# A running sum per token in DRAM in place of a scatter buffer that is read back, in a decoder layer with a mixture of experts

## The reference, cut to what matters

```python
C = int(1.25 * S / E)                                   # 320
topk_pn = topk_p / jnp.sum(topk_p, axis=1, keepdims=True)
idx = buf[:, :C]; valid = idx < S                       # the tokens of each expert
xin = x_pad[idx]
h = jax.nn.relu(jnp.einsum('ecd,edh->ech', xin, w1) + b1[:, None, :])
out = jnp.einsum('ech,ehd->ecd', h, w2) + b2[:, None, :]
out = out * jnp.where(valid, tok_w, 0.0)[:, :, None]
final = jnp.zeros((S + 1, d), xf.dtype).at[idx.reshape(-1)].add(out.reshape(-1, d))[:S]
```

## Time and profile before

| | us |
|---|---|
| median of the runs (lowest, highest) | 564.18 (563.95, 564.62) |
| span of the profiled execution | 558.4 |
| PE, DVE, ACT, POOL busy | 447.8, 374.0, 247.2, 145.5 |
| expert stage, 410 to 495: PE, DVE, ACT, POOL busy | 82.4, 69.7, 77.2, 34.7 |
| last stage, 526 to 558: DVE, ACT, POOL busy | 17.8, 12.2, 17.3 |

### The profile page before, as it was taken

One profiled execution on the slowest core, in us unless ns is written; L12 is line 12 of the kernel. 1 busy time (PEld: TensorE's weight loads), 2 busy tenths in 40 slices (PEclk: granted clock), 3 DMA queues, 4 the chain that ended last, 5 costly groups with the idle time before them and its releaser, 6 DMA issues.

```text
span 558.4 us, 14892 instructions
## 1 busy us (share of the span) xinstructions
PE 447.8 (80%) x5408; PEld 353.1 (63%) x5408; DVE 374.0 (67%) x1572; ACT 247.2 (44%) x802; POOL 145.5 (26%) x207
## 2 busy tenths in 40 slices
PE   4989999898998998998989967621799999999100
PEld 3546777786886877877877856611567777777100
DVE  3656789557658666576575583678578898887074
ACT  0543366224223233233242232442399888883044
POOL 0121351113103102112121131104403444422475
PEclk9979799669559687586595585665699999999755
DMA  8940063110200100100101000010644555500292
GB/s 253 321 161 1 30 210 122 29 31 2 75 0 26 49 0 28 47 0 28 47 0 45 26 1 21 2 39 18 197 155 147 164 166 163 179 25 25 87 312 96
DMA packets 38241, 46.47 MB, mean 83 GB/s; under 512 B 4283, under 2 KB 32702, under 8 KB 38202
## 3 DMA queue, kind: packets, MB, share of 16 engines
q1 hardware_dynamic: 35002, 36.56, 20.4%
q0 software_dynamic: 3200, 9.40, 5.2%
HBM read 34.98 MB, written 11.01 MB: 82 GB/s over the span
## 4 chain that ended last, share of the span: by engine, by line
PE 48%; DVE 20%; ACT 14%; issue 10%; POOL 3%; DMA 2%; SPq 1%; ACTq 1%; DVEq 0%; POOLq 0%
PE bank L748 46%; ACT qp L566 3%; DVE ub L1098 2%; DVE h L1109 2%; ACT arena L657 2%; ACT kp L666 2%; ACT arena L666 2%; DVE h L1112 1%; DVE hist L1110 1%; DVE st L1173 1%; DVE tm L1141 1%; PE bank L1023 1%; DVE mb L1100 1%; ACT arena L695 1%; ACT nb L544 1%
## 5 line engine op out<-in xcount | busy, mean ns | idle before, releaser
L1098 DVE TENSOR_TENSOR_SCAN ub<-rzb,bank 128x32 f32<-128x32 f32 x128 | 28.0, 219 | 90.1 <-ACT rzb L541 89.4
L541 ACT ACTIVATE rzb<-bank 128x32 f32<-128x32 f32 x128 | 27.5, 215 | 131.8 <-PE bank L748 131.8
L748 PE MATMUL bank<-h,whp 128*128 128x16 f16 x1920 | 75.5, 176 | 4.0 <-DVE h L1112 2.6
L748 PEld LDWEIGHTS bank<-h,whp 128*128 128x128 bf16 x1920 | 61.0, 99 | 10.4 <-DVE h L1112 3.3
L748 PEld LDWEIGHTS bank<-hsb,at_w 66*64 66x64 f32 x256 | 31.9, 167 | 43.8 <-DVE hsb L1104 27.3
L748 PE MATMUL bank<-arena 128*128 128x320 f16 x384 | 57.3, 308 | 1.4 <-DVE arena L1488 1.4
L748 PE MATMUL bank<-arena,kp 128*128 128x320 f16 x384 | 54.5, 299 | 0.0
L748 PE MATMUL bank<-hsb,at_w 66*64 66x16 f32 x256 | 41.6, 240 | 14.0 <-DVE hsb L1104 14.0
L748 PEld LDWEIGHTS bank<-arena 128*128 128x128 f16 x384 | 38.3, 102 | 17.0 <-DVE arena L1488 1.6
L544 ACT ACTIVATE nb<-ub 128x16 f32<-128x16 f32 x128 | 27.9, 218 | 43.8 <-DVE ub L1098 43.8
L748 PEld LDWEIGHTS bank<-arena,kp 128*128 128x128 f16 x384 | 37.3, 98 | 14.1
(11 more groups left out here) (203 smaller groups left out, 992.4 us busy)
## 6 DMA issues: line engine op xcount, KB each, us to landing
wbuf<-in_w SPq DMA_DIRECT2D x16, 1024.0 KB
ybuf<-zero POOLq DMA_DIRECT2D x8, 512.0 KB, 7.6
wbuf<-ybuf SPq DMA_DIRECT2D x16, 256.0 KB, 5.8
xin_t<-in_xT SPq DMA_DIRECT2D x16, 128.0 KB, 2.3
arena<-in_ctxT SPq DMA_DIRECT2D x4, 512.0 KB, 7.5
xfin_t<-in_xT SPq DMA_DIRECT2D x16, 128.0 KB, 2.3
xres<-in_xtok SPq DMA_DIRECT2D x16, 128.0 KB, 2.1
x_d<-x SPq DMA_DIRECT2D x8, 256.0 KB, 2.4
```

The lines of the kernel that those rows point to most:

```text
L541: nc.scalar.activation(od(rzb[:]), RZ[j][:, s * 2 * B:(s + 1) * 2 * B], ACT.Sigmoid).then_inc(q["r_ready"], 1)
L748: return nc.tensor.matmul(out_, lhsT, rhs, start=start, stop=stop, skip_group_check=True)
L1098: nc.vector.tensor_tensor_scan(ub[:], rzb[:, 0:2 * B], NS[j][:, s * 32:s * 32 + 32], 0.0, ALU.mult, ALU.add).then_inc(q["npre_ready"], 1)
```

## The change

`ybuf` is gone, and with it the zero fill, the read-back of two rows for each token, the weights `wt` and the sums of the last stage. In its place stands `acc_d`, one row for each token, which starts as a second copy of x2. The routing weight of each token for each of the eight experts is formed on VectorE (`weights`), and stored behind the token's row in `x2_d`, whose rows grow from 256 to 264 numbers; so the gather of an expert's rows brings the weights with it, and GpSimd copies the expert's column out (`slot_weights`). For each expert the sums of its tokens are gathered from `acc_d` (`gather_sums`, after the scatter of the expert before has landed), VectorE multiplies the result by the slot's weight and adds it to the gathered sum on the way out of PSUM (`results`), and the scatter writes the sum back.

The last stage does not wait for the last expert: when the scatters of experts 0 to 6 have landed, SyncE loads all of `acc_d` in eight loads, VectorE takes the statistics of all chunks, GpSimd raises them to the power in two halves, ScalarE normalises in place, the first four chunks before the output of expert 7 and the last four after it, and SyncE stores. The rows of expert 7 are added, normalised by themselves (`st4` to `nm4`), and scattered over the output once all stores have landed. For the last expert TensorE's transposes of the previous result and VectorE's `results` are moved from the second half of the expert to its first.

```diff
+                sp.dma_start(acc_d[bass.ds(2 * c * P, 2 * P), :].rearrange("(k p) d -> p k d", p=P), x2[:, bass.ds(2 * c, 2), :]).then_inc(q["acc_st"], 16)
...
-            for j in range(2):
-                sp.wait_ge(q[f"yst{j}"], 16 * CT * (E // 2))
-            y_v = ybuf.rearrange("(j k p) d -> p j k d", j=2, p=P)
+            sp.wait_ge(q["yst0"], 16 * CT * (E // 2))
+            sp.wait_ge(q["yst1"], 16 * CT * (E // 2 - 1))
             for c in range(CHUNKS):
-                for j in range(2):
-                    sp.dma_start(yg[c][:, 2 * j:2 * j + 2, :], y_v[:, j, 2 * c:2 * c + 2, :]).then_inc(q[f"yl{c}"], 16)
+                sp.dma_start(at[c], acc_d[2 * c * P:2 * (c + 1) * P, :].rearrange("(k p) d -> p k d", p=P)).then_inc(q[f"yl{c}"], 16)
...
@@ gpsimd
+            def slot_weights(e):
+                pool.wait_ge(q[f"xe{e % 2}"], 16 * CT * (e // 2 + 1))
+                pool.tensor_copy(yw[:, e * CT:e * CT + 2], xe[e % 2][:, 0:2, D + e]).then_inc(q["yw_ready"], 1)
+                pool.tensor_copy(yw[0:CAP - 2 * P, e * CT + 2:e * CT + 3], xe[e % 2][0:CAP - 2 * P, 2, D + e:D + e + 1]).then_inc(q["yw_ready"], 1)
+            def gather_sums(e):
+                if e >= 1:
+                    pool.wait_ge(q[f"yst{(e - 1) % 2}"], 16 * CT * ((e - 1) // 2 + 1))
+                for c, m, col in slots(e):
+                    pool.indirect_dma_start(
+                        yt[e % 2][0:m, c, :], None, acc_d[:, :], bass.IndirectOffsetOnAxis(ap=gix[0:m, col], axis=0),
+                        bounds_check=S - 1, oob_is_err=False).then_inc(q[f"yg{e % 2}"], 16)
...
             for e in range(E):
+                slot_weights(e)
                 if e + 1 < E:
                     norms(e + 1)
                 if e + 2 < E:
                     gather(e + 2)
                 if e >= 1:
+                    gather_sums(e - 1)
                     scatter(e - 1)
-            scatter(E - 1)
+            gather_sums(E - 1)
...
+            rstd_3(0)
+            rstd_3(1)
+            pool.wait_ge(q["var4"], 1)
...
+            pool.wait_ge(q["ost"], 16 * CHUNKS)
+            for c, m, col in slots(E - 1):
+                pool.wait_ge(q["f_ready"], c + 1)
+                pool.indirect_dma_start(
+                    out[:, :], bass.IndirectOffsetOnAxis(ap=six[0:m, col], axis=0), yt[(E - 1) % 2][0:m, c, :], None,
+                    bounds_check=S - 1, oob_is_err=False).then_inc(q["fst"], 16)
@@ scalar
+            for c in range(CHUNKS // 2):
+                normalized(c)
+            expert_out(E - 1, 1)
+            for c in range(CHUNKS // 2, CHUNKS):
+                normalized(c)
+            act.wait_ge(q["rstd4"], 1)
...
@@ tensor
-                mm(ps[:, 0:E * CT], lo1[:, n, :], hit[:, n, :], n == 0, False)
-                if n >= TILES:
-                    last = mm(ps[:, 64:64 + E * CT], lo1[:, n, :], hi1[:, n, :], False, n == 2 * TILES - 1)
+                last = mm(ps[:, 0:E * CT], lo1[:, n, :], hit[:, n, :], n == 0, n == 2 * TILES - 1)
...
+                    if f == 2 and last_:
+                        pe.wait_ge(q["yt_ready"], 2 * e - 2)
+                        results_T(e - 1)
@@ vector
+            def weights(a, b):
+                t = slice(a, b)
+                then(nc.vector.tensor_tensor(wsum[:, t], top[:, t, 0], top[:, t, 1], ALU.add))
+                then(nc.vector.reciprocal(wsum[:, t], wsum[:, t]))
+                nc.vector.tensor_tensor(wte[:, t, :], pe_[:, t, :], wsum[:, t].unsqueeze(2).to_broadcast([P, b - a, E]), ALU.mult).then_inc(q["wt_ready"], 1)
...
             ret_low(c)
+            weights(0, TILES - 4)
...
             norm_2(c, 1)
+            weights(TILES - 4, TILES)
...
-            def results(e, j, stored):
+            def results(e, j, i):
                 dve.wait_ge(q["ytr_ready"], e + 1)
-                if stored is not None:
-                    dve.wait_ge(q[f"yst{j}"], stored)
-                nc.vector.tensor_copy(yt[j][:, 0:2, :], bank[0][:].rearrange("p (c d) -> p c d", c=2)).then_inc(q["yt_ready"], 1)
-                nc.vector.tensor_copy(yt[j][0:CAP - 2 * P, 2, :], bank[1][0:CAP - 2 * P, 0:D]).then_inc(q["yt_ready"], 1)
+                dve.wait_ge(q["yw_ready"], 2 * e + 2)
+                dve.wait_ge(q[f"yg{j}"], 16 * CT * (i + 1))
+                for c in range(CT):
+                    m = min(P, CAP - c * P)
+                    w = c * D
+                    last = nc.vector.scalar_tensor_tensor(yt[j][0:m, c, :], bank[w // 512][0:m, w % 512:w % 512 + D],
+                                                          yw[0:m, bass.ds(e * CT + c, 1)], yt[j][0:m, c, :], ALU.mult, ALU.add)
+                    if c >= 1:
+                        last.then_inc(q["yt_ready"], 1)
...
+                    if f == 4 and last:
+                        results(e - 1, 1 - j, i)
```

188 lines of the change are left out of this document (91 added, 97 removed).

## The result

The changed kernel takes 592.2 us (median of four, 590.96 to 594.14) against 564.07 for the kernel before in the same session: a ratio of 1.053, 95% interval 1.048 to 1.059 (the quotient of the two medians is 1.050, inside it). The forecast was 567.0 and its range ended at 573.5: the direction was right, the size far off. The profiled execution has a span of 592.3, against 558.4, and took 594.14, so only 1.8 us lie outside the span; by the same 1.8, the 5.8 us that the prediction carried were 1.8 of that kind and 4.0 by which the profiled execution of before lay under the median. This does not touch the forecast of a difference, but it makes the two traces differ by 33.9 us where the medians differ by 28.1.

A forecast was written before the change was run, and what follows sets the result against it. The prediction took a ring on GpSimd to set the expert period: 8.3 us lost by S(5) at 514.8, plus a tail of 46.5, gives span 561.3; with 5.8 outside it 567.1, rounded to 567.0, range 561.0 to 573.5.

The forecast's parts named there:

- the ring: Expert loop, one first scatter to the next: scatters, power, gathers, landing, add and hand-over in sequence take 16.57 us, against 15.18.
- the meeting with the weight load: Third gather of sums sharing DMA engines with the next weight load, in three periods: 0 to 3.1 us each, taken 0.5.
- GpSimd's issues: Expert loop: three gathers of sums take 2.72 us from first start to third start, as in the earlier trace.
- the tail's gain of 5.4 us: From expert 5's first scatter to the end: 46.5 us, against 51.9 before.
- The bound of the kernel before: Expert loop: TensorE, ScalarE and VectorE form a ring with little room; GpSimd idles 6.84 us a period, off the path.
- a floor of 15.9: VectorE's own path in each expert period, which holds even with an instantaneous gather and decides the fifth period.
- S(5): Start of expert 5's first scatter, S(e) being that of expert e: forecast at 514.8, against 506.46 before.
- rival C: Expert loop: the weight load holds up the third gather by the whole 3.1 us, giving 574.9; chance 0.2.
- S(0) = 431.1: Front, up to expert 0's first scatter: 430.63 before, plus 0.5, less 0.3, plus 0.28.
- rival D: Tail: expert 7 really computes beside the bulk, saving at most some 4 us, giving 563; chance 0.03.
- B: Expert loop: the gather of sums is hidden and VectorE's 15.9 is the period, giving 562.9 or 560.9; chance 0.22.
- 18 or more is C: Sign in the profile after: first scatters 18 us or more apart mid-loop would show the load holding up the gather.

The follow-up runs named there:

- e4: The kernel before, with three more gathers into a spare buffer in each GpSimd iteration, waited for only by the next such gathers: 563.4 us, ratio 1.003.
- e10: The kernel of e2 with VectorE's split of the weights cut to 32 columns from expert 2 on (output not the reference's): 565.4 us.
- e12: The kernel of e11 with each weight load cut into eight 256 KB transfers, one behind each of VectorE's eight splits of hidden rows: 568.6 us, ratio 1.015.
- e1: The changed kernel with the weight loads of experts 2 to 7 cut to 1/64 (stale weights): 577.7 us.
- e2: The changed kernel with whole weight loads issued only when the sums (first load: expert 0's rows) have landed: 577.3 us, ratio 1.024.
- e5: The changed kernel with sums gathered before rows, the load issued when expert e+1's rows have landed, and the power ahead of the slot copies: 582.0 us, ratio 1.041.
- e3: The changed kernel with GpSimd gathering the sums before the rows of expert e+2: 581.3 us, ratio 1.034.
- e9: The changed kernel with sums gathered first, later loads issued when the last sums have landed, and expert 7's bias step before the bulk norms: 575.5 us, ratio 1.023.
- e7: The kernel of e5 with ScalarE's bias step of expert 7 ahead of the first half of the bulk norms: 582.0 us, ratio 1.037.
- e8: The kernel of e5 without the three last scatters of expert 7's rows over the output, which lacks those rows: 576.8 us.
- e6: The kernel of e5 with the overlap at the end undone: expert 7 adds and scatters, then the bulk is loaded and normalised: 579.6 us, ratio 1.031.
- e11: The kernel of e9 with the bulk norms of chunks 4 to 7 on VectorE instead of ScalarE: 574.6 us, ratio 1.022.

## Why the prediction was wrong, step by step

In short, two terms of the ring were sized too low (the meeting with the weight load, 0.5 for a measured 2.5 to 3.4 us, and GpSimd's issues, 1.5 to 2.6 us a period over their rows), the same meeting was left out at the front (5.5 us), and the tail's gain of 5.4 us did not come.

**The bound of the kernel before** held. The gap on GpSimd was real (e4 fills it with three gathers at no cost), and "issue, landing, add and hand-over together do not" fit was right.

**The ring.** Its structure was right, and so were its terms where nothing disturbs them: 16.54 in e10 against 16.57, 15.5 in the changed kernel for the period without rows against a floor of 15.9 (its terms add up to 15.84), 13.6 from S(5) to S(6) against 13.2. Two terms were mis-sized.

The first is the meeting with the weight load, "0 to 3.1 us a period; I take 0.5", on the ground that only 64 rows meet a load that has just begun. It measured 3.3, 3.4 and 2.5 in the three periods (in the first, 4.95 against 1.66 from issue to add), and this is rival C's size, about the top of the bounds from the earlier trace rows. The reason given for the low choice, how few rows are asked for, did not hold: the traces show instead that the two 1 MB loads fill all DMA engines (98% busy, 335 GB/s) for 6 to 7 us once they have begun. By the Trainium skill (DMA: Bandwidth & Descriptors, Queues, rings and completion order), cited in the prediction against its own choice, an engine drains a packet of one queue before it turns to the next. The cost does lie where the prediction said that this rule would put it. In e12 the same bytes go as small transfers, the DMA engines are 89% busy, and the gathers beside them are held up less (4.4 to 5.2 us from issue to landing against 6.9); that it is the packets that do this wasn't tested.

The second is the price of an issue. All terms with GpSimd's issues took 0.95 to 1.09 us from the earlier trace rows, where gathers are issued while VectorE handles hidden rows. The added gathers fall 4 us later, beside VectorE's 4.9 us split of the weights, and there 2.03 is common. That is 0.3 or 0.4 for the first two (1.2 where one of them doubles too), 1.1 for the third and 0.2 to 0.7 ahead of them, copies and power included: 1.5 to 2.6 a period, in no rival. No row of before has an indirect issue in that stretch of the loop; at its front one lies beside such a split and took 0.95 (389.93), so the rows shown could not have warned of it, but neither did the prediction name the neighbour. It took a duration from one place of the period and used it in another.

Rival C gave 574.9: the first cause alone, in three periods. Both together, in the three periods with a load, make 65.5 - 51.2 = 14.3 us over the forecast (9.2 of waiting beside the load, where 1.5 was allowed, and 6.8 of GpSimd's own list, less 0.3 by which the undisturbed landing is shorter than its row); in S(3) to S(4) the second alone makes 1.4.

**The front**, "S(0) = 431.1". Here a step was left out. The load of weights for expert 2 stands in SP's queue near the first gathers, and expert 0's sums are gathered just when the next load runs. The prediction gave the collision to "three periods" and asked for no other place where a waited-for gather and a load meet. There were two more, and the piece grew by 3.4 and 3.5 us there. The load is most of it: without it or with it held back the piece is 45.0 (e1) and 45.2 (e2) instead of 50.6. The rest is stretched issues: with the split shortened as well it is 43.0 (e10), and with the load held back and the sums ahead of the rows 43.6 (e5), as in the kernel before. "The three old weight operations went beside the gather: nothing" was part of it, since they had kept the split, and with it the load, further behind the first gather. The small edits ahead of the first gather did cost little: from GpSimd's last `qr` operation (351.20 before, 353.77 after) to that gather it is 35.95 us before and 36.10 after, where 0.2 more was forecast (36.0 to 37.1 in all twelve traces with that front).

**Why the waits add up to so much.** The prediction saw the ring, but not that a longer ring moves every transfer in it. e3, e5 and e9 each take the load off one transfer and put it on another: sums, scatter, rows. Before the change only the rows were waited for in the loop, and with some 7 us in hand (a last issue ends at 469.35, its rows are used at 478.67, and 1.8 of that is the landing).

**The tail**, forecast 46.5, measured 52.9 (relative to S(5)):
- bulk loads at 19.9, not 18.0: 1.4 of it is the first issue of expert 6's scatter, 2.39 instead of 1.03, beside VectorE's splits of hidden rows; 0.4 the later S(6).
- power ready at 30.4, not 27.2: 1.9 inherited, and 1.2 because "the loads keep up" was wrong. The third chunk made VectorE wait 1.23 us, while the gather of expert 7's sums ran beside the bulk loads. The power on 8 columns, 1.67 with 2.5 for the four operations, was as reckoned.
- from there to the last scatter 15.4 (30.4 to 45.8), as forecast (27.2 to 42.6). That ScalarE's first half stands before expert 7's output was seen, and rival D priced undoing it at 4; it gave 1.5 (e7), where ScalarE's norms and the last store lead the chain.
- behind the last scatter 7.1 us, not 3.9: about 3.1 more at the program's end, where the last wait is 4.8 (1.4 before) and the prediction had carried over "1.7 to the end". It is 4.0 without the last scatters (e8) and 2.7 with the plain tail (e6). What makes it so long stays open.

So the tail's gain of 5.4 was eaten by terms of 1 to 3 us each, and e6 puts the gain of the whole overlap at 0.4. My reading, not tested: as long as each scatter waits for the landing of the one before it, the bulk can't start early enough to hide much.

**The rivals and the range.** B was refuted (the adds wait for data in every period). The range ended at 573.5 although C, a chance of 0.2, stood at 574.9, and it took each rival alone; an unpriced collision times four or five places is what it had to hold. **The signs** announced in the prediction did their work: "18 or more is C" is what the scatters showed, TensorE's idle time was 4.6 instead of 1 to 2, and the clock fell as it said it might. The timelines show little cost of that fall by itself: the ring ran through GpSimd and the DMA engines, and GpSimd waits 0.24 us for TensorE ahead of its gather of rows, where 0.20 stood before. In e9 and e12 the clock is back at 1.00.

## What to carry to other kernels

Before a transfer is put on the path, ask at every place of its use what else is on the DMA engines then: here a gather of 64 rows lands 1.7 us after its issue alone and 5 to 6 us beside a load that fills the engines. If three transfers of a loop are waited for, moving the bulk load only changes which of them it hits; cutting it into pieces paced by the compute, which also moved it, did better here (S(0) to S(5) is 81.5 us in e12, against 84.8 and 87.1 in e9 and e11 with whole loads). And take an instruction's duration from a row with the same neighbours on the other engines, not only of the same shape; a read-modify-write through DRAM in each turn of a loop costs issue, landing, add, issue and landing in sequence, which was worth 0.4 us of overlap at the end and cost 1.4 us a period or more even undisturbed (e10).

## What the runs showed of the hardware

- GpSimd issued an indirect DMA in 0.92 to 1.16 us where VectorE ran neither split (303 issues in the fourteen traces). Beside the split of the weights, `scalar_tensor_tensor` on two SBUF operands, 100 of 244 took 1.8 to 2.2 us, and the others down to 0.94 (the issue at 389.93 of the earlier trace rows is one); what decides between them stays open. With that operation shortened, the gathers of the sums of experts 0 to 4 took 0.94 to 1.05 (e10). Beside the split of hidden rows, `tensor_tensor` on two SBUF operands, 343 of 354 took 0.92 to 1.43, and 11, all the first issue of expert 6's scatter, 2.39. The Trainium skill (SBUF — State Buffer, Who interferes with whom) says that a VectorE instruction with two SBUF inputs contends with a GpSimd instruction that reads SBUF. The runs agree for the split of the weights; the many undisturbed issues beside the split of hidden rows show that two SBUF inputs alone don't settle it.
- Two loads of 1 MB took the DMA engines to 98 to 103% busy and 335 to 372 GB/s, and a scatter or gather of 320 rows beside them landed 3 to 4.5 us later (1.7 to 5.0, 2.2 to 5.5, 1.7 to 6.2 us after its last issue).
- Eight transfers of 256 KB kept the DMA engines at 89% and 299 GB/s over 5 us, and the gathers beside them took 4.4 to 5.2 us from issue to landing, against 6.1 to 7.0 for the third gather beside the 1 MB loads and 3.0 to 3.6 without a load.
- VectorE normalises 256 columns in 0.33 us with a multiply and add by per-row scalars, ScalarE in 0.50.
